# Scores of a second cross-attention: masked fp32 products against one-pass products of stacked high and low parts

## What is computed

```python
q = proj(query, Wq, bq)        # (8, 16, 112, 16)
k = proj(key, Wk, bk)          # (8, 16, 375, 16)
v = proj(value, Wv, bv)
attn = jnp.einsum('bhqd,bhkd->bhqk', q, k) / jnp.sqrt(jnp.float32(Dh))
attn = jax.nn.softmax(attn, axis=-1)
out = jnp.einsum('bhqk,bhkd->bhqd', attn, v)
```

## Time and profile before

| | us |
|---|---|
| three runs | 739.29, 743.01, 743.85 (median 743.01) |
| the profiled execution, own time | 738.25 |
| its span | 736.4 |
| TensorE busy | 710.7 (97%) |
| VectorE busy | 542.2 (74%) |
| ScalarE busy | 451.9 (61%) |
| GpSimd busy | 193.6 (26%) |
| chain that ended last: PE / DVE / ACT / issue | 80% / 11% / 3% / 3% |
| scores, line 1989 (256 instructions in all) | 471.7 to 609.3 |

### The profile page before, as it was taken

The page is one execution under the profiler, slowest core; times in us unless marked ns, Lnnn a source line. Parts: engine busy times, 40 slices in busy tenths (PEclk is TensorE's granted clock), DMA queues, the critical chain, the costliest instruction groups (busy, mean ns, idle before and its releaser), DMA issues.

```text
span 736.4 us, 16122 instructions
## 1 busy us (share of the span) xinstructions
PE 710.7 (97%) x5674; PEld 594.5 (81%) x5674; DVE 542.2 (74%) x1285; ACT 451.9 (61%) x1218; POOL 193.6 (26%) x319
## 2 busy tenths in 40 slices
PE   9999999999998999999999999889999999999998
PEld 8567777777776788999999999766776767888988
DVE  2798788888687320777787887978887895897754
ACT  3677677677657513677777795677877796112131
POOL 4132231210000043011001207664464546201000
PEclk9999999999999999999999999999999999999999
DMA  5322234333110478477666522420000000000001
GB/s 171 99 78 74 73 103 116 96 102 91 42 36 20 146 247 301 137 257 251 223 220 216 201 92 77 152 103 3 2 2 2 2 3 1 1 1 1 0 7 45
DMA packets 43571, 69.84 MB, mean 95 GB/s; under 512 B 6643, under 2 KB 35068, under 8 KB 43236
## 3 DMA queue, kind: packets, MB, share of 16 engines
q1 hardware_dynamic: 41956, 65.15, 27.7%
q0 software_dynamic: 1536, 3.67, 1.5%
HBM read 52.57 MB, written 8.26 MB: 83 GB/s over the span
## 4 chain that ended last, share of the span: by engine, by line
PE 80%; DVE 11%; ACT 3%; issue 3%; DMA 1%; POOL 1%; SPq 0%; POOLq 0%; ACTq 0%; DVEq 0%
PE ps L1605 13%; PE ps L1880 10%; PE ps L1897 8%; PE ps L2111 7%; PE ps L1677 5%; PE ps L1674 5%; PE ps L1716 4%; PE ps L1736 4%; PE ps L1989 3%; PE ps L1804 3%; PE ps L1610 2%; PE ps L2146 2%; PE ps L1687 2%; PE ps L1793 2%; PE ps L2024 2%
## 5 line engine op out<-in xcount | busy, mean ns | idle before, releaser
L1605 PEld LDWEIGHTS ps<-ident,arena 112*122 112x122 f32 (+5 forms) x584 | 64.2, 155 | 28.6 <-issue 14.5
L1605 PE MATMUL ps<-ident,arena 112*122 112x112 f32 (+5 forms) x584 | 82.3, 276 | 5.1 <-ACT rt L909 3.4
L845 ACT ACTIVATE arena_r<-ps,bt 128x128 fp32r<-128x128 f32 x168 | 70.1, 419 | 17.9 <-PE ps L1880 17.9
L1880 PE MATMUL ps<-OT,arena 128*128 128x128 f32 x672 | 78.5, 275 | 0.6 <-issue 0.6
L2111 PE MATMUL ps<-arena_r 128*112 128x384 f32 x384 | 76.7, 348 | 1.9 <-DVE acc L1392 1.0
L1880 PEld LDWEIGHTS ps<-OT,arena 128*128 128x128 f32 x672 | 76.7, 192 | 0.9 <-issue 0.8
L1084 DVE TENSOR_REDUCE negmax<-ps 112x1 f32<-112x375 f32 x128 | 61.1, 539 | 21.0 <-PE ps L1989 20.9
L846 ACT ACTIVATE OT<-ps,bt 128x128 f32<-128x128 f32 x168 | 71.1, 425 | 0.0
L2111 PEld LDWEIGHTS ps<-arena_r 128*112 128x112 f32 x384 | 64.5, 177 | 4.2 <-DVE arena L1527 1.2
L1079 DVE TENSOR_REDUCE negmax<-ps 112x1 f32<-112x487 f32 x64 | 39.4, 658 | 20.3 <-PE ps L1716 19.6
L704 ACT ACTIVATE arena<-ps,negmax 112x487 f32<-112x487 f32 x64 | 42.8, 671 | 16.7 <-DVE negmax L1079 16.7
(11 more groups left out here) (344 smaller groups left out, 1732.8 us busy)
## 6 DMA issues: line engine op xcount, KB each, us to landing
arena<-in_up_w SPq DMA_DIRECT2D x21, 1024.0 KB, 4.9
arena<-in_down_w SPq DMA_DIRECT2D x8, 1024.0 KB, 7.0
arena<-arena SPq DMA_DIRECT2D x128, 60.9 KB, 2.0
arena<-in_wqkv SPq DMA_DIRECT2D x1, 3072.0 KB, 11.0
arena<-in_ctx SPq DMA_DIRECT2D x8, 375.0 KB
slot_rows<-acc SPq DMA_DIRECT2D x6, 448.0 KB, 3.5
OT<-slot_rows SPq DMA_DIRECT2D x21, 128.0 KB, 2.6
slot_out<-yo SPq DMA_DIRECT2D x21, 128.0 KB, 2.6
```

Of the source, the lines that this page charges most:

```text
L845: act.activation(he_hi[:, i % 2, m, :], src, ACT.Gelu, bias=bt[:, i % 3, m:m + 1])
L1605: return pe.transpose(dst, src, ident[0:k, 0:k])
L1880: ins = pe.matmul(ps[:, 2 * (i % 2) + m // 4, (m % 4) * SLOT:(m % 4 + 1) * SLOT], wu[i % 2][:, c, m * P:(m + 1) * P], xgT[:, i % 2, c, :], ...
```

## The change

A head's score is computed from parts of less precision: Q = Qhi + Qlo and K = Khi + Klo. In place of zeros, the 16 idle rows of a tile now hold the low part of the same head's K: for the even heads of a pair (index o = 0) rows 0 to 15 hold Khi and rows 16 to 31 Klo, for the odd heads the other way round. Q's parts stand in both halves. Then Qhi times the stack is Qhi Khi + Qhi Klo, and a second product with Qlo adds the rest. Both are one-pass (fp32r) products, so a step has eight of them where it had four fp32 products.

To get there, each batch's K is cast twice (`k_st`, o = 0 and 1), its low part is subtracted, and eight DMAs move low parts over 16 partitions into the other halves; the same is done for Q (`q_st`, eight DMAs). Batches 2 to 7 are cast and subtracted on GpSimd (`k_parts`, `q_parts`). For batches 0 and 1 ScalarE writes the two casts straight from PSUM, and VectorE makes the low part (`k_low`) and Q's parts. The mask of heads is gone. Q of batch 0 is taken after batch 4's combination in place of 5's, Q of batch 1 ahead of the first scores, and the load of `wqkv` moves behind the stack of batch 6.

```diff
@@ block.sync @@
+            def k_stack(n):
+                sp.wait_ge(s_kp, n + 1)
+                if n:
+                    sp.wait_ge(s_kst, 128 * n)
+                for o in (0, 1):
+                    for at in range(16 * o, P, 32):
+                        sp.dma_start(k_st[n][at ^ 16:(at ^ 16) + 16, o, :, 0:TK].bitcast(F32), kT_lo[n][at:at + 16].bitcast(F32))                          .then_inc(s_kst, 16)
...
+            k_stack(0)
             sp.wait_ge(s_kve, 4 * NEAR)
             sp.dma_start(wo1, a["o_proj"].rearrange("(k p) n -> p k n", p=P)).then_inc(s_wF, 16)
-            sp.wait_ge(s_mnorm, B)
-            sp.dma_start(wqkv, a["wqkv"].rearrange("(c p) e n -> p c e n", p=P)).then_inc(s_wF, 16)
+            q_stack(0)
+            for n in range(1, B):
+                k_stack(n)
+                q_stack(n)
+                if n == 6:
+                    sp.wait_ge(L1["s"], 5 * H1)
+                    sp.dma_start(wqkv, a["wqkv"].rearrange("(c p) e n -> p c e n", p=P)).then_inc(s_wF, 16)
@@ block.gpsimd @@
-            def q_heads(n):
+            def k_parts(n):
+                pool.wait_ge(s_kve, 4 * n + 2)
+                if n in (2, 3, 4, 7):
+                    pool.wait_ge(L1["s"], (n - 1) * H1)
+                if n in (5, 6):
+                    pool.wait_ge(s_kst, 128 * n)
+                if n in (3, 5, 6):
+                    k_pad(n)
+                for o in (0, 1):
+                    ins = pool.tensor_copy(k_st[n][:, o, :, 0:TK], kT[n])
+                link(ins)
+                pool.tensor_tensor(kT_lo[n], kT[n], k_st[n][:, 0, :, 0:TK].bitcast(F32), ALU.subtract).then_inc(s_kp, 1)
+
+            def q_parts(n):
+                pool.wait_ge(s_qt, (n + 1) * KC)
                 if n >= 2:
                     pool.wait_ge(L1["s"], (n - 1) * H1)
...
+                for o in (0, 1):
+                    ins = pool.tensor_copy(q_st[n % 2][:, o, 0], qt)
+                link(ins)
+                for o in (0, 1):
+                    ins = pool.tensor_tensor(q_st[n % 2][:, o, 1], qt, q_st[n % 2][:, o, 0].bitcast(F32), ALU.subtract)
+                ins.then_inc(L1["qe"], 1)
...
             for n in range(1, B):
                 if n + 1 < B:
-                    q_heads(n + 1)
+                    k_parts(n + 1)
+                    q_parts(n + 1)
@@ block.scalar @@
             def k_out(n):
                 for k in range(KC):
                     act.wait_ge(s_kv, 4 * n + k + 1)
+                    if n < 2:
+                        for o in (0, 1):
+                            act.activation(k_st[n][:, o, k, 0:TK], ps[:, k, 0:TK], ACT.Identity, bias=b1[:, 1, k:k + 1])
@@ block.vector @@
+            def k_low(n):
+                dve.wait_ge(s_kve, 4 * n + 2)
+                dve.tensor_tensor(kT_lo[n], kT[n], k_st[n][:, 0, :, 0:TK].bitcast(F32), ALU.subtract).then_inc(s_kp, 1)
...
-                if b == B - 3:
+                if b == B - 4:
                     l1_q(0, 0)
-                if b == B - 2:
-                    q_heads0(0)
+                    q_parts(0)
+
+            l1_q(1, 1)
@@ block.tensor @@
-                for i in range(4):
-                    h, rows = HEADS[4 * v + i], slice(32 * i, 32 * i + 32)
-                    pe.matmul(ps[0:TQ, S_BANKS[i], 0:TK], qm[n % 2][rows, h, :], kT[rows, n, h // 8, :],
-                              start=True, stop=True, tile_position=(32 * i, 0)).then_inc(L1["s"], 1)
-
+                for k in (0, 1):
+                    for i in range(4):
+                        rows = slice(32 * i, 32 * i + 32)
+                        ins = pe.matmul(ps[0:TQ, S_BANKS[i], 0:TKP], q_st[n % 2][rows, v % 2, k, v // 2, :],
+                                        k_st[n][rows, v % 2, v // 2, :], start=(k == 0), stop=(k == 1),
+                                        tile_position=(32 * i, 0))
+                        if k:
+                            ins.then_inc(L1["s"], 1)
```

87 lines of the change are left out of this document (51 added, 36 removed).

## The result

| | before | changed |
|---|---|---|
| median (lowest to highest) | 742.1 us (739.3 to 744.3) | 745.9 us (740.3 to 750.8) |
| executions | 20 | 20 |
| profiled execution, its span | 738.25 us, 736.4 us | 748.08 us, 746.2 us |
| mean granted clock of that span | 0.995 | 0.979 |

The ratio is 1.0058, with an interval of 1.0038 to 1.0079: the changed kernel is a little slower. On two other chips it was 1.0033 (1.0012 to 1.0054) and 1.0071 (1.0044 to 1.0097). The forecast was 742.6 us, no change; 745.9 lies in its range of 735 to 751 and inside the 1% band, but the sign was missed.

What follows compares the result with a forecast made beforehand. The prediction saw equal VectorE and TensorE chains bounding the steady steps, and VectorE the beginning. Terms -8.7, +3.0 and +5.3 gave -0.4 us, so 742.6 us carried to the median; range 735 to 751.

Steps and rivals of the forecast that it cites:

- (g): Beginning: batch 1's Q bias ahead of the first maximum, +0.55 us; batch 0's Q parts and their DMAs charged nothing.
- The product, 0.31 us a step: Score steps: eight one-pass products take about 0.59 us instead of 0.90; 28 times 0.31 gives -8.7 us.
- (a): Steady part: steps where VectorE is already full gain nothing, some five of the last eleven; +0.9 us.
- (d): Steady part: VectorE instructions reading two SBUF operands stand while GpSimd's two-operand ones run; +0.9 us (0 to 3).
- Rival 3: Score steps: one-pass products in row tiles don't run side by side, +0.65 us per step, about 769 us; chance 4%.
- the rule against the order: Score products: weight loads overlap only products of another row group, so the gain would be some 5 instead of 8.7 us.
- (b): Batches 2 to 7: GpSimd's parts and SP's stacking DMAs take 15.5 of 17.3 us, hidden with 1.8 us to spare.
- Rival 2: Batches 2 to 7: the stack becomes the bound, 748.5 to 757 us; chance 18%.
- (c): Batch 5: its scores wait for the stack because GpSimd inverts the norms first, 2.93 us; +1.2 us (to 3.5).
- (e): Beginning: ScalarE writes the first two batches' K three times, delaying context 6's high part, for which VectorE waits; +1.75 us.
- (f): Beginning: the low part of batch 0's K goes ahead of VectorE's row combinations; +1.0 us.
- (h): Behind the first maxima: VectorE makes batch 1's parts under GpSimd's spreads, delaying the second maximum; +2.0 us (0.8 to 3.2).

Runs made afterwards that it cites:

- e2_fill: Changed kernel plus 17 idle products in TensorE's two gaps of the first steps, into bank 4, overwriting transposed rows of batches 6 and 7; 741.1 us, ratio 1.0005.
- e15_fill_bank5: Changed kernel plus 17 idle products in TensorE's two gaps between the first steps, into a bank where they overwrite nothing; 743.9 us, ratio 1.0012.
- e16_changed_again: Changed kernel, untouched, measured again; 747.6 us, ratio 1.0071 to the kernel before.
- e5_stack_late: Changed kernel with the eight stacking DMAs of batch 0's keys issued behind the o_proj load instead of ahead; 744.2 us, ratio 1.0047.
- e7_tile_by_tile: Changed kernel with a score step's eight products reordered, both products of a row tile one behind the other; 745.2 us, ratio 1.0052.
- e10_q_after_5: Changed kernel with batch 0's query bias and parts back behind row combination 5 instead of 4; 742.8 us, ratio 1.0000.
- e1_again: Changed kernel, untouched, run and profiled again; 744.5 us, ratio 1.0033 to the kernel before.
- e12_before_again: Kernel before, untouched, for a second profile of it; 741.8 us, ratio 1.0007.

## Why the prediction was right or wrong

**The step that failed.** The forecast rests on TensorE's full clock, "granted through this stretch", and its sum has no term for the lower level. The two windows of rows 1 leave out 478 to 504, and there before's own profile shows it:

```profile
478.00:482.00 4.00, 4.00 (x26) 3.57 (x18) 3.96 (x7) 2.60 (x8) 3.85 (x8) 0.57 1.01 430
```

In its place the runs showed the 1.2 GHz level for 10 to 17 us in the first steps of all ten profiles of the changed kernel and its variants without idle products, worth 2.1 to 4.4 us by the medians of e2_fill and e15_fill_bank5, and 2.2 us of it in batch 4. Beside it, (g) charged nothing for a wait that was there. The terms in turn:

**The product, 0.31 us a step: right.** 0.60 us by the timeline where 0.57 to 0.62 was given. From s(1, 0) to s(4, 0) a step took 4.02 us instead of 4.30, 0.28 less; 27 steps took 114.1 instead of 117.0, where 111 was said, with (a) to (d) already in it. Against 27 times 0.31 the change gave back 5.5 us: 3.9 in batch 4 and 1.6 in the other 23 steps, 0.07 each. Rival 3 and the rule against the order are out.

**(a) and the steps of batches 5 to 7: right in kind.** 11 steps gained 2.1 us where 11 times 0.31 is 3.4: 1.3 given back, 0.9 said for the full steps and a part of (d).

**(b), the stack in time: right.** K's two casts took 1.56 and the subtraction 1.65, 3.2 us against 4.0 reckoned. Eight issues of K took 5.10 us. Batch 4's data landed near 553.1 (545.75, 5.40 for eight issues, 1.9 to land) and its scores started at 554.45, 1.4 us to spare where 1.8 was said. Rival 2 did not come.

**(c) and (d), batch 4: the step that was mis-sized.** The prediction had 1.2 us for the stack of batch 5 and 0.9 for all contention. It charged the norms' 2.93 us only to the DMAs. The same delay moves GpSimd's subtraction from a place beside VectorE's maxima, which does not disturb them, onto the copy of the inverted sums; with the gate constants behind it the maxima are 1.4 us late, which TensorE shows as 1.20 us idle. Without the clock that makes 2.0 us over four steps of 4.0 (e16_changed_again), near the 2.1 of (c) and (d) together, but in other shares: 0.6 for the stack, and none in the first profile of the change, where the scores of batch 5 waited for no DMA. With the clock it is 4.2: its 2.2 were not in the sum.

**(e) and (f): right.** The first combination started 13.1 us after the first key product instead of 10.4, +2.7 where 1.75 and 1.0 were said (450.2 forecast; 454.0 less the 4.0 us by which everything was later).

**(g): wrong.** "Batch 0's Q parts stand for the masked products: nothing" compared durations and not places. The change puts the bias, which waits for TensorE, behind batch 4 instead of batch 5. Where ScalarE and TensorE run free this costs nothing (e5_stack_late, e7_tile_by_tile: VectorE does not wait, and 41.1 us to the first maximum are +3.5 for the 3.4 forecast). Where ScalarE stalls, and it does in nearly every profile of both kernels, VectorE waits, 2.4 us in the first profile of the change. e10_q_after_5 puts the bias back: the wait falls to 0.73 us and the median by some 0.3 to 0.7%. The first profile of before, on which all was built, was the one without the stall.

**(h): right in place, too dear in itself, short in consequence.** k_low(1) took 2.11 us under GpSimd's spread, casts and subtractions 2.0; the second maximum came 5.8 us after the first where 5.4 was before, and 6.5 in e1_again: +0.4 to +1.1 where +2.0 was charged. That was worked out as a delay of VectorE. Not worked out was that TensorE, 3.17 us idle, then runs the next two steps at 1.2 GHz. Before has less of it: in its first profile one gap of 3.26 us and the lower level for some 4 us behind it, in the second two gaps of 1.34 and 1.40 us and none.

**The sum.** Steps -8.7, (a) to (d) +3.0, (e) to (h) +5.3 gave -0.4. Taking the clock's share away leaves about that: e15_fill_bank5, in which the first steps keep the clock but batch 4 does not, stands at 1.0012, where -0.4 us would be 0.9995. The error is what the prediction's sum had no term for: the clock around the gaps, some 2 to 4 us in the first steps (e2_fill, e15_fill_bank5) and 2.2 in batch 4, and the place of one wait. That the remaining terms add up so closely is partly luck: (h) was charged 0.9 to 1.6 us too much, (g) nothing for its wait. The base was 0.9 us high as well: 743.0 is the median of three executions, 742.1 that of twenty.

## What to carry to other kernels

A step that was made cheaper gave its gain here only while TensorE stayed fed: when a change lengthens a gap on TensorE, add to the sum the next steps at 1.2 GHz, read off how much longer the same instructions take there, and try idle products in the gap before judging the change. Compare the place of every wait, not only the duration of the work behind it: one row combination more between a product and its reader was worth some 0.3 to 0.7%. And take two profiles of the kernel before: the first one here missed two waits that every other profile of both kernels shows.

## What the runs showed of the hardware

- ScalarE stood for 1.6 to 6.2 us at a time, mostly with its inputs ready, between 450 and 461, in every profile but the first of before, in both kernels, whatever the stacking DMAs did. It is marked as issue, remote or with a product that had ended long ago. Its cause stays open.
- A gap of 1.20 us on TensorE at the same place in batch 4 was followed by the 1.2 GHz level for some 7 us in eight profiles and by none in e16_changed_again. In the first steps of the changed order without idle products there are two gaps, of 1.0 to 2.3 and 2.7 to 3.8 us, and the lower level came each time: in five of ten profiles within or at the start of the longer one, in the other five 0.2 to 3.4 us before it, so the length of that gap alone does not decide it. Two gaps of 1.34 and 1.40 us (e12_before_again) and two of 1.16 and 1.15 (e15_fill_bank5) brought none.
- Eight one-pass products in four 32-row tiles took 0.60 and 0.61 us in the two orders, with all weight loads in 0.29.
- VectorE's copy of 256 elements from one input took 0.29 to 0.78 us, 1.66 while GpSimd subtracted 750 elements with two inputs and 1.12 beside its subtraction of 384; maxima read from PSUM beside the same subtraction kept their 1.91. The Trainium skill, "GPSIMD Engine Reference", section 1, names contention for VectorE instructions with two SBUF inputs or in a two-port mode; the copy has one input, and no run shows its mode.
